# Attention on one core: fc1 part 2 and fc2 issued in the next step, the fourth exponential ahead of the gelus, PSUM banks in another rotation

## The reference

```python
xn = _layernorm(xt, norm1_g, norm1_b)                 # over 48 channels
xw = windows of 7 x 7 tokens of roll(xn, (-3, -3))    # N = 49 tokens
qkv = (xw @ qkv_w + qkv_b)                            # 3 heads, dh = 16
attn = einsum('bhnd,bhmd->bhnm', q, k) * dh ** -0.5
attn = softmax(attn + bias, axis=-1)
out = einsum('bhnm,bhmd->bhnd', attn, v) @ proj_w + proj_b
x = x + windows and roll undone
xn = _layernorm(x, norm2_g, norm2_b)
h = gelu(xn @ fc1_w + fc1_b) @ fc2_w + fc2_b          # 48 -> 192 -> 48
x = x + h
```

## Time and profile before

| | |
|---|---|
| median of three runs | 1989.23 us |
| the profiled execution | 1988.41 us |
| its span | 1986.8 us |
| mean granted TensorE clock | 0.954 of full speed |
| PE busy | 1758.4 us, 89% of the span |
| ACT busy | 1537.5 us, 77% |
| DVE busy | 1364.4 us, 69% |
| POOL busy | 1174.5 us, 59% |

### The profile page before, as it was taken

The page is one execution under the profiler, slowest core; times in us unless marked ns, Lnnn a source line. Parts: engine busy times, 40 slices in busy tenths (PEclk is TensorE's granted clock), DMA queues, the critical chain, the costliest instruction groups (busy, mean ns, idle before and its releaser), DMA issues. The chain is left out here.

```text
span 1986.8 us, 90056 instructions
## 1 busy us (share of the span) xinstructions
PE 1758.4 (89%) x38074; PEld 1076.0 (54%) x38074; DVE 1364.4 (69%) x2007; ACT 1537.5 (77%) x2890; POOL 1174.5 (59%) x1048
## 2 busy tenths in 40 slices
PE   4999999999999999999999999984899958999994
PEld 2666666565656566565656566641597933333331
DVE  7776767676767677676767677543677757888872
ACT  3788888888888888888888888863566639889880
POOL 5687877777777778777786877641255540222222
PEclk9999999999999999999999999985799975999998
DMA  3343554444434444343444444312388759999983
GB/s 111 97 105 104 142 133 103 104 109 101 113 99 115 99 108 107 99 103 100 115 99 112 102 109 99 75 44 65 101 216 214 217 123 177 241 263 258 259 229 111
DMA packets 233226, 262.24 MB, mean 132 GB/s; under 512 B 167078, under 2 KB 179910, under 8 KB 232710
## 3 DMA queue, kind: packets, MB, share of 16 engines
q1 hardware_dynamic: 217478, 217.50, 44.8%
q0 software_dynamic: 15360, 39.08, 6.6%
HBM read 160.82 MB, written 80.88 MB: 122 GB/s over the span
## 5 line engine op out<-in xcount | busy, mean ns | idle before, releaser
L416 POOL TENSOR_TENSOR shift<-const_b,qmax 113x588 bf16<-113x588 bf16 x256 | 299.8, 1171 | 224.6 <-DVE qmax L511 224.5
L563 DVE TENSOR_TENSOR x<-ps_m,x 112x392 f32<-112x392 f32 x128 | 66.5, 562 | 269.6 <-PE ps_m L1012 269.6
L511 DVE TENSOR_REDUCE qmax<-ps_s 113x12 f32<-113x588 f32 x256 | 194.9, 761 | 67.4 <-PE ps_s L891 67.2
L1472 POOL DMA_DIRECT2D out_rolled<-r_OUT x128 | 64.0, 504 | 280.5 <-DVE r_OUT L1572 280.5
L700 ACT ACTIVATE P<-ps_t 113x588 f32<-113x588 f32 x256 | 172.0, 672 | 54.2 <-PE ps_t L943 53.5
L732 ACT ACTIVATE G<-ps_m 128x392 f32<-128x392 f32 x384 | 178.2, 500 | 41.0 <-PE ps_m L993 40.5
L1324 PE MATMUL conv_ps<-xin,band_now 64*64 64x448 bf16 x2688 | 203.3, 365 | 4.1 <-DVE x_low L1226 4.1
L503 DVE TENSOR_TENSOR Ul<-Uf 113x784 bf16<-113x784 f32 x192 | 204.9, 1094 | 0.0
L406 POOL TENSOR_TENSOR xhl<-xh 113x784 bf16<-113x784 f32 x64 | 203.5, 3180 | 2.2 <-DVE xh L551 2.2
L693 ACT COPY Uf<-ps_m 113x392 f32<-113x392 f32 x384 | 172.9, 486 | 32.4 <-PE ps_m L858 24.5
L1324 PE MATMUL conv_ps<-x_low,band_now 64*64 64x448 bf16 x1344 | 179.9, 352 | 0.0
(11 more groups left out here) (241 smaller groups left out, 5192.3 us busy)
## 6 DMA issues: line engine op xcount, KB each, us to landing
xin<-rows_scratch SPq DMA_DIRECT2D x96, 236.0 KB, 3.7
XT<-x_tokens SPq DMA_DIRECT2D x64, 294.0 KB, 3.2
X<-x_windows SPq DMA_DIRECT2D x128, 147.0 KB, 3.3
RS<-rs_scratch SPq DMA_DIRECT2D x128, 147.0 KB, 3.4
XR<-x_windows SPq DMA_DIRECT2D x128, 147.0 KB, 3.1
x_scratch<-x SPq DMA_DIRECT2D x128, 147.0 KB, 3.3
y_scratch<-y POOLq DMA_DIRECT2D x96, 196.0 KB, 2.8
r_RS<-rs_scratch SPq DMA_DIRECT2D x128, 147.0 KB, 4.5
```

Of the source, the lines that this page charges most:

```text
L416: nc.gpsimd.tensor_tensor(shift[:, j % 2], e, m, ALU.mult).then_inc(S["md"], 1)
L511: nc.vector.tensor_reduce(qmax[:, j % 2, :].rearrange("p (b n) -> p b n", b=2), ps_s[0:R, :, 0:2 * HQ].rearrange("p b (n t) -> p b n t", t ...
```

## The change

TensorE: `fc1(., 2)` and `fc2` of a strip are no longer issued at the end of the step in which `fc1(., 0)` and `fc1(., 1)` are, but early in the next one, around `variance` of the following strip; one more step is run at the end. `weigh(s, 2)` moves between `fc1(old, 0)` and `fc1(old, 1)`. `keys_and_values` and `key_bias` of quad 0 move from the front of the step to the end of the step before. `shift_scores(s, 3)` moves ahead of `fc1(old, 0)`. ScalarE: `exp_scores(s, 3)` and `keep_values(s, 3)` stand ahead of the table load for the gelus and no longer behind or among them; `square(prv)` is third in the block and not second. VectorE: `second_residual` behind the token sums, `divide(s, 1)` ahead of `u_low(nxt, 2)`. GpSimd: `make_shift(s, 2)` ahead of `wrap_columns`. `BANKS` gives each use another pair. No instruction is added or taken away.

```diff
--- before.py
+++ after.py
@@ -40,8 +40,8 @@
 GRING = 2
 TLEAD = 5
 HRING = 3
-BANKS = {"var": (0, 1), ("u", 0): (2, 0), "proj": (1, 2), ("u", 1): (0, 1), ("u", 2): (2, 0), "cen": (2, 0),
-         ("f1", 0): (1, 2), ("f1", 1): (0, 1), ("f1", 2): (2, 0), "f2": (1, 2)}
+BANKS = {("f1", 2): (0, 1), "var": (2, 0), "f2": (1, 2), ("u", 0): (0, 1), "proj": (2, 0), ("u", 1): (1, 2),
+         ("u", 2): (0, 1), "cen": (0, 1), ("f1", 0): (2, 0), ("f1", 1): (1, 2)}
 
 
 def columns(*widths):
@@ -443,8 +443,8 @@
             def step(s):
                 old, prv, nxt, nx2 = s.at(-2), s.at(-1), s.at(1), s.at(2)
                 make_shift(s, 1)
+                make_shift(s, 2)
                 wrap_columns(s.at(-3))
-                make_shift(s, 2)
                 make_shift(s, 3)
                 x1_low(prv)
                 low1(old)
@@ -567,11 +567,11 @@
 
             def step(s):
                 old, prv, nxt, nx2 = s.at(-2), s.at(-1), s.at(1), s.at(2)
-                second_residual(s.at(-3))
+                query_max(s, 2)
                 divide(prv, 2)
-                query_max(s, 2)
                 token_sums(s.at(4))
                 token_squares(s.at(3))
+                second_residual(s.at(-3))
                 divide(prv, 3)
                 normalise0(nx2)
                 query_max(s, 3)
@@ -581,9 +581,9 @@
                 u_low(nxt, 0)
                 u_low(nxt, 1)
                 subtract_mean(prv)
+                divide(s, 1)
                 u_low(nxt, 2)
                 query_max(nxt, 0)
-                divide(s, 1)
                 query_max(nxt, 1)
 
             def clear_inputs(tiles, r):
@@ -759,19 +759,19 @@
                 token_root(s.at(3))
                 invert_sums(s, 1)
                 invert_sums_end(s, 1)
+                exp_scores(s, 3)
+                keep_values(s, 3)
                 if old.real:
                     nc.scalar.preload_act_table_set("gelu_and_others")
                 gelu(old, 0, 0)
+                gelu(old, 0, 1)
                 square(prv)
-                gelu(old, 0, 1)
                 gelu(old, 1, 0)
-                keep_values(s, 3)
                 gelu(old, 1, 1)
                 gelu(old, 2, 0)
                 gelu(old, 2, 1)
                 if old.real:
                     nc.scalar.preload_act_table_set("natural_log_exp_and_others")
-                exp_scores(s, 3)
 
             act.wait_ge(eps_made, 1)
             nc.scalar.preload_act_table_set("natural_log_exp_and_others")
@@ -1016,16 +1016,12 @@
             def step(s):
                 old, prv, nxt = s.at(-2), s.at(-1), s.at(1)
                 before = s.at(-3)
-                if before.real:
-                    taken(("f1", 2), 1, S["ge"], 6 * before.n + 6)
-                    for b in range(2):
-                        taken("f2", b, S["x2_made"], 2 * before.n + b + 1)
-                keys_and_values(s, 0)
-                key_bias(s, 0)
                 query_bias(s, 2)
                 query_scores(s, 2)
                 shift_scores(s, 0)
+                fc1(before, 2)
                 variance(old)
+                fc2(before)
                 weigh(prv, 3)
                 u_product(nxt, 0)
                 keys_and_values(s, 1)
@@ -1046,16 +1042,16 @@
                 key_bias(s, 3)
                 query_bias(nxt, 0)
                 query_scores(nxt, 0)
+                shift_scores(s, 3)
                 fc1(old, 0)
-                shift_scores(s, 3)
-                fc1(old, 1)
+                weigh(s, 2)
                 query_bias(nxt, 1)
                 query_scores(nxt, 1)
-                fc1(old, 2)
-                weigh(s, 2)
-                fc2(old)
-
-            steps(step, -1, N + 2)
+                keys_and_values(nxt, 0)
+                key_bias(nxt, 0)
+                fc1(old, 1)
+
+            steps(step, -1, N + 3)
```

## The result

The changed kernel takes 2400.39 us (median of four runs, 2376.91 to 2411.21) against 1989.29 us before (four runs). The ratio estimated from all the runs is 1.202, with a 95% interval of 1.197 to 1.207; the two medians alone give 1.207. The kernel is slower by 20%. The forecast was 2309 us, with a range up to 2400: two of the four runs lie inside the range, and the median is 0.4 us above its end. 320 us of loss were forecast, 411 came.

What follows compares the result with a forecast made beforehand. PE's call order was taken to bound the kernel. Bank waits of 3.56 us plus 1.6 of clock make 5.16 us a step, times 62 is 320 us on top of 1988.4: 2309 us against the median, range 2195 to 2400.

Steps and rivals of the forecast that it cites:

- The bank waits: New bank rotation on PE: fc2 half 1 waits 3.0 us for log_variance(old, 0), u 0 about 1.0 for log_variance(old, 1).
- t = 11.89: Time in us within a step, counted from the start of keys_and_values(s, 3) on PE at t = 0.
- The term of 3.56 us a step: Step period computed as 23.65 us against 20.09 with the new bank waits, before any loss of clock.
- The old waits: fc1 on PE waiting for a gelu, 1.0 us a step before; claimed to shrink to about 0.3, or some 0.5.
- The clock term: PE's clock drops to 1.2 GHz behind the new stalls; taken as 1.6 us a step, bounds 0 and 2.9.
- the row with one clean gap: Profile before: PE idle 1.68 us at 67.3, then half clock until about 72.4, priced at 1.6 us.
- The rival of long spells: Slow clock spells on PE of 2.9 us in each step, 2390 us; chance 0.15.
- That the clock holds: Rival: the stalls come but PE stays at 2.4 GHz, 2210 us; chance 0.17.
- That only the second wait is real: Rival: ACT reaches log_variance(old, 0) in time, only u 0's wait counts, + 0.56 us a step, 2024 us; chance 0.06.
- the faster side: Rival: gelu waits are covered and neither new bank wait is felt, 56 us less, 1933 us; chance 0.05.
- Costed at nothing: Moved second_residual, divide and make_shift taken to lie beside PE work at no cost; at most 1.5 us a step.
- `variance`, said to have its squares in time: variance on PE needs POOL's low half of the squares; claimed not to be the late one.

Runs made afterwards that it cites:

- filled_both: Changed kernel plus 20 extra matmuls ahead of fc2's first matmul and 7 ahead of u 0, results overwritten, all waits kept: 2234.24 us, ratio 1.120.
- logs_first: Changed kernel with both log_variance calls first on ScalarE behind the table load, ahead of invert_sums, token_square and the exponential: 2126.05 us, ratio 1.065.
- banks_alone: Kernel before with the new bank table alone, nothing moved: 2058.43 us, ratio 1.031.
- fc2_first_filled: Changed kernel, fc2 ahead of variance with their banks swapped, second_residual ahead of token sums, 9 extra matmuls while PE waits for the last gelu: 2077.87 us, ratio 1.042.
- filled_fc2: Changed kernel with the 20 extra matmuls ahead of fc2 alone, gap before u 0 left empty: 2233.36 us, ratio 1.118.
- exp_ahead: Kernel before with the change's front half alone (exp_scores, keep_values, shift_scores of quad 3, weigh(s, 2), divide(s, 1) moved): 2229.41 us, ratio 1.119.
- filled_u0: Changed kernel with the 7 extra matmuls before u 0 alone, gap in fc2 left empty: 2297.47 us, ratio 1.151.
- logs_resid: Changed kernel with both log_variance calls first behind ScalarE's table load and second_residual ahead of the token sums on VectorE: 2112.02 us, ratio 1.061.

## Why the prediction was right, and where it was off

- **The bank waits were right in place and releaser, and in length to within 0.3 us.** `fc2` stops in its middle for `log_variance(old, 0)`: resumed at t = 11.89, computed 11.86. `u 0` waits for `log_variance(old, 1)`: 1.0 us. The step with a held clock is 23.75 us, computed 23.65. `logs_first` shows that the position of the two logarithms causes most of the loss, 274 of 411 us; `banks_alone` gives the second wait by itself with 1.03 us. The term of 3.56 us a step is 3.9 us when read from the times of `filled_both`, 0.35 more than computed. The trace shows where: from one `project` to the next, 22 of 42 steps have 23.73 to 23.76 us and the others up to 27.2; the mean is 24.16, against 20.26 before. Why those are longer is open.
- **The old waits shrank as said**: from 1.0 us a step to 0.25 (9.3 us in 38 steps), against 0.3 to 0.5.
- **The clock term was mis-sized, and it is not what it was said to be.** The step that failed is "I take 1.6, the row with one clean gap", for each step. It measured 2.7 us a step on average (`filled_both` against the changed kernel). The trace of the changed kernel shows no step of that size: 14 of 38 lose next to nothing, and the other 24 have 3.4 to 6.7 us more than 23.75. One reason for the larger price is shown: the row with one clean gap had nothing behind it, while here the second gap falls into the slow spell and lengthens it. The long gap alone costs 1.0 us a step on average, both together 2.7. Why the same gap brings the clock down in one step and not in another is open.
- **The range held by a rival's number.** The rival of long spells, with its 2390 us and a chance of 0.15, comes nearest. Its price of 2.9 us in each step is near the average of 2.7, but the mixture above is not its mechanism; that the two numbers meet is luck. The forecast of 2309 itself fell 91 us short.
- **Rivals.** That the clock holds is what `filled_both` makes artificially: 2234 us, where that rival said 2210. The changed kernel itself does it in 14 steps of 38. That only the second wait is real is `banks_alone` in the order of before. No run of the half-step move came out on the faster side; the best one, `fc2_first_filled`, is still 4% slower than before.
- **Costed at nothing:** the later `second_residual`, `divide` and `make_shift`. In the changed kernel PE waited 6.2 us for VectorE in 1000 us (4.3 for `query_max`, 1.9 for `subtract_mean`) and never for `make_shift`, so this is nearly right. `logs_first` shows that it holds only for this order: there `second_residual` became the last releaser, with a wait of 1.26 us. `variance`, said to have its squares in time, waited for `squares_low` in 30 of 38 steps, 13.2 us in all; that is on PE ahead of `fc2`, whose second half waits for the logarithm in any case.

## What to carry to other kernels

With a few PSUM banks in rotation, write down for each use which instruction reads the bank before it and what that reader stands behind on its own engine; a move by half a step changes all of these pairs at once. Move a reader that sits behind a table load to the front (`logs_first`), or, which no run here tests by itself, give its bank to the user that comes last. A stall of PE costs its length and then the clock behind it: price both, and look whether a second, shorter gap follows in the slow spell. Where a call needs two banks, let its first half go with the first bank.

## What the hardware showed that I had not expected

- A gap of 1.0 us before `u 0` leaves the clock at 0.97 to 1.00 when it is alone (`banks_alone`, `filled_fc2`), and costs 1.7 us a step on average where the long gap is open too. Behind gaps of 1.25, 0.5 and 1.0 us in close order the clock was down in each step (`exp_ahead`, 0.88). The same gap of 2.6 us brought it down in one step and not in its neighbour (`filled_u0`; 22 of 38 second halves in the changed kernel).
- Matmuls whose result nobody reads saved 166 us of 2400, 7%.
- `u_low` on VectorE and `low1` on GpSimd, run side by side: 1.85 us for two and 3.26, or 3.40 for two and 2.22. The Trainium skill, page "SBUF — State Buffer", section "SBUF: two separate sides", says that the two engines share a pair of ports, also where the VectorE operation has two inputs in SBUF as `u_low` has, and that the one which comes first holds it for its whole instruction. The row of `logs_resid` fits such a lock: the pair of `u_low` starts first, and it ends at 641.49, 0.83 us after `low1` (640.66), about the length of one `u_low` (1.85 for two). The kernel before doesn't fit it as well: there `low1` starts 0.06 us ahead of the pair and still is the one that is longer. No run here separates the lock from another cause.
